# Attention kernel: both halves' weighted values together, projection in the fourth score bank

## What is computed

```python
def reference(x, ...):                      # x: (32, 96, 16, 16), float32
    x = _L0_conv_ref(x, ...)                # windowed attention, then an MLP
    return _L1_conv_ref(x, ...)             # channel attention

def _L0_conv_ref(x, qkv_w, qkv_b, proj_w, proj_b, rel_bias, ...):
    xn = _layernorm(x, norm1_g, norm1_b)    # over the 96 channels
    xs = jnp.roll(xn, shift=(-SS, -SS), axis=(1, 2))
    qkv = (xw @ qkv_w + qkv_b)...           # xw: 4 windows of 64 tokens per image, 12 heads of 8
    attn = jnp.einsum('bhnd,bhmd->bhnm', q * SCALE, k) + bias + mask
    attn = jax.nn.softmax(attn, axis=-1)
    out = jnp.einsum('bhnm,bhmd->bhnd', attn, v)...
    out = out @ proj_w + proj_b
    x = shortcut + jnp.roll(xs, shift=(SS, SS), axis=(1, 2))
    h = _layernorm(x, norm2_g, norm2_b)
    h = jax.nn.gelu(h @ fc1_w + fc1_b, approximate=False)
    return x + (h @ fc2_w + fc2_b)

def _L1_conv_ref(...):                      # layer norm over the image, 3x3 grouped convolutions
    ...                                     # to Q, K, V, 8 heads of 12 channels, softmax over
                                            # channels, a 1x1 projection and the normalised x
```

## Time and profile before

| | before |
|---|---|
| median of 3 executions | 552.92 us (550.82 to 564.15) |
| the profiled execution | 551.77 us, of which span 549.8 us |
| PE busy | 505.5 us (92%) |
| DVE busy | 337.8 us (61%) |
| ACT busy | 310.2 us (56%) |
| POOL busy | 176.7 us (32%) |
| mean granted TensorE clock | 0.97 of full speed |

### The profile page before, as it was taken

How to read it: one execution, slowest core, us unless ns; L and a number is a source line. 1 busy time by engine, 2 the same in 40 slices (tenths; PEclk the granted TensorE clock), 3 DMA queues, 4 the chain that set the end, 5 groups by cost and what they waited for, 6 DMA issues and landing times. The chain is left out here.

```text
span 549.8 us, 27773 instructions
## 1 busy us (share of the span) xinstructions
PE 505.5 (92%) x11496; PEld 337.2 (61%) x11496; DVE 337.8 (61%) x875; ACT 310.2 (56%) x763; POOL 176.7 (32%) x217
## 2 busy tenths in 40 slices
PE   7789999999999999999799999939999999999996
PEld 6767667667666666767575433219665565656553
DVE  1158888888888888887602473356456656566544
ACT  1138888888888888886533655302444444444432
POOL 8224444443333344444220202003353323333200
PEclk9779999999999999999999999977999999999998
DMA  3111111111111111100031132322464444434411
GB/s 76 25 49 33 32 31 42 26 26 25 29 29 29 29 29 29 29 4 4 1 82 37 39 88 66 96 61 55 113 167 112 110 121 118 113 105 114 120 50 30
DMA packets 40899, 32.62 MB, mean 59 GB/s; under 512 B 18954, under 2 KB 36491, under 8 KB 40843
## 3 DMA queue, kind: packets, MB, share of 16 engines
q1 hardware_dynamic: 37258, 26.11, 18.8%
q0 software_dynamic: 3584, 5.72, 4.7%
HBM read 18.36 MB, written 7.13 MB: 46 GB/s over the span
## 5 line engine op out<-in xcount | busy, mean ns | idle before, releaser
L391 POOL TENSOR_TENSOR scores<-scores,peak 128x768 f32<-128x768 f32 x64 | 92.9, 1473 | 148.1 <-DVE peak L555 148.1
L1235 POOL DMA_DIRECT2D x_stack<-padded_x x96 | 52.4, 548 | 96.3 <-PE ps_v L1508 59.8
L454 ACT COPY probs_t<-ps_probs 128x768 f32<-128x768 f32 x64 | 51.1, 799 | 18.8 <-PE ps_out L733 9.4
L548 DVE TENSOR_TENSOR scores<-ps_scores,bias 128x1536 f32<-128x1536 f32 x32 | 55.3, 1727 | 6.3 <-PE ps_scores L706 6.2
L716 PE MATMUL ps_probs<-ident,scores 128*128 128x128 f32 x384 | 55.9, 282 | 0.1
L555 DVE TENSOR_REDUCE peak<-scores 128x24 f32<-128x1536 f32 x32 | 55.8, 1744 | 0.1
L448 ACT ACTIVATE scores<-scores 128x768 f32<-128x768 f32 x64 | 54.2, 847 | 0.4 <-POOL scores L391 0.4
L733 PE MATMUL ps_out<-v_blocks,probs_t 128*32 128x18 f32 x3072 | 38.9, 187 | 15.2 <-DVE stream L574 15.1
L733 PEld LDWEIGHTS ps_out<-v_blocks,probs_t 128*32 128x32 f32 x3072 | 32.5, 110 | 31.5 <-issue 17.6
L1048 ACT ACTIVATE hidden<-ps_hidden,fc_b_folded 128x512 f32<-128x512 f32 x48 | 29.1, 688 | 36.5 <-PE ps_hidden L989 36.5
L1508 PE MATMUL ps_qk<-x_stack,conv_w 40*32 40x256 f32 x1536 | 48.8, 379 | 0.0
(11 more groups left out here) (159 smaller groups left out, 907.2 us busy)
## 6 DMA issues: line engine op xcount, KB each, us to landing
x_stack<-padded_x SPq DMA_DIRECT2D x96, 54.0 KB
x_stack<-padded_x POOLq DMA_DIRECT2D x96, 54.0 KB, 2.8
padded_x<-x_pad SPq DMA_DIRECT2D x32, 121.5 KB, 2.7
x_sliced<-stream SPq DMA_DIRECT2D x48, 64.0 KB, 2.0
mixed<-y_sliced SPq DMA_DIRECT2D x48, 64.0 KB, 2.0
out<-y_sb SPq DMA_DIRECT2D x32, 96.0 KB, 2.0
x_now<-in_x SPq DMA_DIRECT2D x32, 72.0 KB, 1.8
stream<-in_x SPq DMA_DIRECT2D x32, 72.0 KB, 1.9
```

What stands on the lines that cost most here:

```text
L391: nc.gpsimd.tensor_tensor(sc, sc, peak[:, par, p, :].unsqueeze(2).to_broadcast((128, HEADS, WN)), ALU.subtract).then_inc(s["shifted"], 1)
L454: nc.scalar.copy(probs_t[:, :], ps_turned).then_inc(s["turned_copied"], 1)
L548: nc.vector.tensor_tensor(scores[:, par, :, :].rearrange("p a (g c) -> p a g c", g=NG), ps_scores[:, :, 0:PAIRS * TRIO * WN].rearrange("p ...
L1235: engine.dma_start(x_stack[64 * half + i * HC:64 * half + (i + 1) * HC, slot, :, :], rows).then_inc(landed[slot], 16)
```

## The change

Five things are edited, all in `window_attention`.

- `probs_t` gets two buffers, one for each pair, and `copy_turned` waits one `weigh` less.
- Both halves of an image's `weigh` stand together at the end of PE's step t - 1, behind `project` and `turn_tokens`. Before, the second half stood in step t behind `score`. `turn_heads(t)` moves up to the place behind the first `turn`.
- `ps_proj` moves to bank 3 of `ps_scores`. With it, `weigh` no longer waits for a residual; `score(t)` waits until `residual_done` has reached t - 2, which in step t is the residual of image t - 1. `project` and `make_v` have further waits for the last images only.
- On DVE, `weigh_heads(t)` moves ahead of `add_bias(t + 2)`. The statistics are taken one step sooner, `measure(t + 5)` behind `copy_k(t + 3)`, and `add_residual(t)` follows them, at the end of step t. Before, the same residual stood near the start of step t + 1.
- On ACT, the second `exponent` moves ahead of the first `copy_turned`, and `copy_ot` ahead of `copy_q`.

The number and the sizes of the compute instructions stay as they are. Only the residual and the projection use another bank.

```diff
--- before.py
+++ after.py
@@ -246,7 +246,7 @@
     v_blocks = sb("v_blocks", [128, 2, PAIRS, 2, HP, 2, VC])
     scores = sb("scores", [128, 2, PAIRS, SC])
     peak = sb("peak", [128, 2, PAIRS, HEADS])
-    probs_t = sb("probs_t", [128, SC])
+    probs_t = sb("probs_t", [128, PAIRS, SC])
     recip = sb("recip", [128, PAIRS, HEADS])
     heads_out = sb("heads_out", [128, PAIRS, C])
     out_t = sb("out_t", [C, 2, N])
@@ -260,7 +260,7 @@
     ps_folded = ps_scores[0:C, 2, 0:3 * C]
     ps_q, ps_k = (ps_scores[:, g, 0:N] for g in range(2))
     ps_v = ps_scores[:, 2, 0:2 * C].rearrange("p (w q d) -> p w q d", w=2 * PAIRS, d=HD)
-    ps_proj = ps_out[0:C, 0, N:2 * N]
+    ps_proj = ps_scores[0:C, 3, 0:N]
     ps_turned = ps_probs.rearrange("p b c -> p (b c)")[:, 0:SC]
     ps_pv = ps_out[:, 0, 0:PAIRS * HEADS * VC].rearrange("p (a h c) -> p a h c", h=HEADS, c=VC)
     ps_ot = ps_out[0:C, 0, N:2 * N].rearrange("p (a n) -> p a n", a=PAIRS)
@@ -450,8 +450,8 @@
         def copy_turned(t, p):
             u = t * 2 + p
             act.wait_ge(s["turned"], u + 1)
-            need(act, s["pv_ready"], u)
-            nc.scalar.copy(probs_t[:, :], ps_turned).then_inc(s["turned_copied"], 1)
+            need(act, s["pv_ready"], u - 1)
+            nc.scalar.copy(probs_t[:, p, :], ps_turned).then_inc(s["turned_copied"], 1)
 
         def copy_ot(t, par):
             act.wait_ge(s["ot_ready"], t + 1)
@@ -473,15 +473,14 @@
                 inverse_deviation(t + 4)
                 scale(t + 4)
             if real(t + 1):
+                exponent(t + 1, 1, 1 - par)
                 copy_turned(t + 1, 0)
             if is_image(t, B - 2):
                 copy_tokens(nc, act, m, s2, 0, by_blocks(first_homes[0]))
-            if real(t + 1):
-                exponent(t + 1, 1, 1 - par)
+            if real(t):
+                copy_ot(t, par)
             if real(t + 3):
                 copy_q(t + 3)
-            if real(t):
-                copy_ot(t, par)
             if real(t + 2):
                 copy_v(t + 2, par)
             if real(t + 4):
@@ -568,7 +567,7 @@
                                     ALU.mult).then_inc(s["heads_ready"], 1)
 
         def add_residual(t, half, par):
-            dve.wait_ge(stream_in[1 - par], half * 32 if par == 0 else (half + 1) * 32)
+            dve.wait_ge(stream_in[par], (half + 1) * 32)
             dve.wait_ge(s["proj_ready"], t + 1)
             dst = stream[:, bass.ds(t * N, N)]
             nc.vector.scalar_tensor_tensor(out=dst, in0=ps_proj, scalar=b_proj[:, 0:1], in1=dst,
@@ -589,21 +588,15 @@
 
         def step(t, half, par):
             if real(t + 4):
-                measure(t + 4)
-                await_stats(t + 4)
-            if real(t - 1):
-                add_residual(t - 1, half, par)
-            if real(t + 4):
                 gather_spread()
             if is_image(t, -4):
                 prepare()
+            if real(t):
+                weigh_heads(t)
             if real(t + 2):
                 add_bias(t + 2, par)
             if is_image(t, B - 2):
                 measure_tokens(nc, dve, m, s2, 0, by_blocks(first_homes[0]))
-            if real(t):
-                weigh_heads(t)
-            if is_image(t, B - 2):
                 measure_tokens(nc, dve, m, s2, 1, by_blocks(first_homes[1]))
             if is_image(t, B - 1):
                 for k in range(QUARTERS, 2 * QUARTERS):
@@ -614,6 +607,11 @@
                 set_up_projection()
             if real(t + 3):
                 copy_k(t + 3)
+            if real(t + 5):
+                measure(t + 5)
+                await_stats(t + 5)
+            if real(t):
+                add_residual(t, half, par)
             if is_image(t, B - 2):
                 measure_tokens(nc, dve, m, s2, 2, by_blocks(first_homes[2]))
                 dve.wait_ge(weights_in, 16 * LATE)
@@ -684,6 +682,8 @@
                              skip_group_check=True).then_inc(s["k_ready"], 1)
 
         def make_v(t, par):
+            if past(t + 1):
+                pe.wait_ge(s["biased"], B)
             heads = w_qkv[:, 2 * WIDE:2 * WIDE + C].rearrange("c (q e d) -> c q e d", e=2, d=HD)
             for window in range(2 * PAIRS):
                 for part in range(PARTS_W):
@@ -696,6 +696,7 @@
 
             pe.wait_ge(s["q_copied"], t + 1)
             need(pe, s["v_copied"], t * 2)
+            need(pe, s["residual_done"], t - 2)
             pe.wait_ge(s["k_copied"], t + 1)
             for p in range(PAIRS):
                 for g in range(NG):
@@ -724,14 +725,12 @@
             if p == 0:
                 pe.wait_ge(s["v_copied"], (t + 1) * 2)
                 need(pe, s["ot_copied"], t * PAIRS)
-            else:
-                need(pe, s["residual_done"], t)
             pe.wait_ge(s["turned_copied"], u + 1)
             for q in range(HP):
                 for part in range(PARTS_W):
                     at = q * 128 + 32 * part
                     mm = nc.tensor.matmul(ps_pv[32 * part:32 * part + 32, p, 2 * q:2 * q + 2, :],
-                                          probs_t[:, at:at + 32], v_blocks[:, par, p, part // 2, q, :, :],
+                                          probs_t[:, p, at:at + 32], v_blocks[:, par, p, part // 2, q, :, :],
                                           start=True, stop=True, skip_group_check=True)
             mm.then_inc(s["pv_ready"], 1)
 
@@ -743,6 +742,8 @@
 
         def project(t, par):
             pe.wait_ge(s["ot_copied"], (t + 1) * PAIRS)
+            if past(t + 2):
+                need(pe, s["residual_done"], t)
             nc.tensor.matmul(ps_proj, w_proj[:, :], out_t[:, par, :], start=True, stop=True,
                              skip_group_check=True).then_inc(s["proj_ready"], 1)
 
@@ -795,10 +796,10 @@
                 score(t + 2)
             if is_image(t, -2):
                 fold_v()
-            if real(t):
-                weigh(t, 1, par)
             if real(t + 1):
                 turn(t + 1, 0, 1 - par)
+            if real(t):
+                turn_heads(t)
             if is_image(t, -4):
                 fill(nc, free, blank[:, :], 8)
             if real(t + 4):
@@ -809,8 +810,6 @@
                 fill(nc, free, blank[:, :], 6)
             if real(t + 3):
                 make_q_and_k(t + 3, 1 - par)
-            if real(t):
-                turn_heads(t)
             if real(t + 2):
                 make_v(t + 2, par)
             if is_image(t, B - 2):
@@ -825,11 +824,13 @@
                 fold_fc1(2)
             if real(t + 1):
                 turn(t + 1, 1, 1 - par)
-                weigh(t + 1, 0, 1 - par)
             if real(t):
                 project(t, par)
             if real(t + 5):
                 turn_tokens(t + 5, half + 2 + par, 1 - par)
+            if real(t + 1):
+                weigh(t + 1, 0, 1 - par)
+                weigh(t + 1, 1, 1 - par)
             if is_image(t, -2):
                 fill(nc, free, blank[:, :], 6)
 
@@ -838,7 +839,7 @@
         fill(nc, free, blank[:, :], 10)
         pe.wait_ge(turning_in, 16)
         led_image_loop(pe, step)
-        fill(nc, ps_scores[0:C, 3, 0:C], blank[:, :], 16)
+        fill(nc, ps_out[0:C, 0, 0:C], blank[:, :], 16)
         for c in range(SLICES):
             turn_first_slice(c)
```

## The result

| | before | after |
|---|---|---|
| median of 4 executions each | 554.5 us (550.82 to 564.15) | 575.62 us (573.45 to 575.79) |
| ratio, 95% interval | | 1.0395 [1.0326, 1.0464] |
| span of the profiled execution | 549.8 us | 573.7 us |
| PE busy | 505.5 us (92%) | 506.0 us (88%) |
| DVE busy | 337.8 us | 344.5 us |

A ratio leaves out executions more than 1.5% above the fastest of their kernel (here the one of 564.15 us), so that it is not the ratio of the two medians.

A forecast was written before the change was run, and what follows sets the result against it. It took a loop over PE and DVE (tokens, statistics, residual, `weigh`) as the bound; loop 6.6, unrolled images 1.6, start 0.7 and end 0.5 sum to 9.4 us more, forecast 561.5 us, range 554 to 568.

The forecast's parts named there:

- The tail: End of windowed attention: MLP statistics stand behind a residual they used to precede; +0.5 us, between -0.3 and +1.
- What bounds the kernel before: Loop before the change: tokens, statistics, residual and `weigh` close a loop over PE and DVE; 7.166 us an image.
- The bubble moves to the bias: Between scores and queries on PE: the 0.54 us wait at `weigh` goes, a new one of at least 0.37 us comes.
- The closed chain: Looped images: scores now wait for the residual behind the statistics; 7.44 us an image against 7.166, 6.6 us in the loop.
- Project to tokens: Chain term on PE, from `project` to `turn_tokens`: 0.51 us.
- Residual to scores: Chain term from DVE's residual, with the way to PE, to the next scores: 0.54 us.
- The signs that the prediction named: Scores wait for the residual some 30 times, about 0.35 us each; queries wait for the bias 0.4 to 0.5 us.
- What hides the rest: In the loop: early `weigh_heads` costs nothing, DVE cover 0.35 us; ACT's turned copy stays hidden, cover 0.27 us.
- The unrolled images: Five steps outside the loop, images 0, 1 and 26 to 28: +0.33 us each, 1.6 us.
- the head: Start of windowed attention: the first image's second `weigh` stands ahead of a score, 0.56 us plus a copy wait; +0.7 us.
- The clock: Rival: two PE bubbles an image bring half clock in the loop, 3 us more an image, over 600 us; chance 0.03.
- The third: Rival: extra conditions and register instructions around scores, bias and reciprocal make 7.65 us an image, 566 us; chance 0.24.

The follow-up runs named there:

- the version with early tokens: Kernel before with tokens' transposes ahead of the first weigh, normed copy ahead of values, statistics sooner, residual and gather ahead of the bias: 549.46 us, ratio 0.9756.
- four costs removed: Changed kernel with residual ahead of statistics, normed copy ahead of values, idle matmuls at the tail, four images per loop turn: 559.16 us, ratio 1.0050.
- the runs without this wait: Changed kernel with the residual ahead of the statistics (565.17 us), and further versions of it, such as four images per loop turn (565.66 us).
- the second weigh back: Changed kernel with PE's order and the reciprocal's place put back, second half's weigh again behind the scores: 583.34 us, ratio 1.0544.
- its long loop: Kernel before with four images in a turn of the loop in place of two: 554.40 us, ratio 1.0008.

## Why the prediction was wrong, step by step

The direction and the chain were right; the sum was 14.4 us short (9.4 for 23.8, both on the profiled executions). Two steps failed. The tail, "+0.5, between -0.3 and +1", measured 5.5: it priced late statistics and not the idle time and the clock behind them. The chain, "The sum is 7.44 us", measured 7.64: `project` to `turn_tokens` and the residual to the scores were too short, 4.7 us over the loop. The start gave 2.2 us more than summed in this profile (in its repeat 1.0 less) and the later stages 2.4 where nothing was put; for these the cause stays open.

**What bounds the kernel before: right.** The loop over tokens, statistics, residual and `weigh` was the limit; the version with early tokens broke it and took 0.23 us from each image (with the statistics sooner and the normed copy first).

**The bubble moves to the bias: right.** Scores to queries was put at 2.92 us; it is 2.91 (107.17 to 110.08). Neither the loss of the cover nor its return (3.00 us) moves it. The Trainium skill, "Perfetto Trace Analysis", section "Optimization Strategy", has repeated bubbles as a possible sign of too few buffers; by the earlier trace rows that rule promised 6.63 us an image. The runs disagree: with both buffers and the fourth bank in place and four costs removed, the image takes 7.206 us. The bubble stood at a buffer, and its cause was an order of instructions.

**The closed chain: right in kind, mis-sized in two terms.** Against the sum, start to start, with the mean over the two kinds of image:

| term | predicted | measured |
|---|---|---|
| scores to queries | 2.92 | 2.91 |
| queries to values | 1.03 | 1.03 |
| values to the second turn | 0.47 | 0.48 |
| turn to project | 0.81 | 0.71 |
| project to tokens | 0.51 | 0.70 |
| tokens to statistics | 0.41 | 0.45 |
| statistics to residual | 0.75 | 0.66 |
| residual to scores | 0.54 | 0.70 |
| sum | 7.44 | 7.64 |

- *Project to tokens, 0.51 us.* The prediction took it from the earlier trace rows as if PE alone decided it. It had the copies on ACT in hand, 0.71 and 0.43 us, and used them for the turned copy only; that `copy_normed` must also free `ps_a` for the tokens it did not ask. The kernel with the normed copy first shows the term: 0.26 us less at the tokens, 0.19 less an image.
- *Residual to scores, 0.54 us.* It was read at a `weigh` in the middle of a step. The scores open the step, and in every second image the turn of the loop as well, where it measures 0.83 us and not 0.58. That the 0.25 more is the loop's branch is an inference from the runs without this wait, where 0.44 to 0.64 us stay before the same images and move with the branch. Before, the same branch lay mostly under other work.

The signs that the prediction named came, and larger than put: the scores wait 27 times for 0.47 us each (0.35), the queries 30 times for 0.77 us (0.4 to 0.5), since PE's work between scores and queries ends after 2.15 us and not 2.55 (107.17 to 109.32).

The two mis-sized terms make 0.35 us, the other six give 0.15 back: 0.20 us an image, 4.7 of the 14.4 us missed.

**What hides the rest: right, and with little to spare.** ACT's turned copy releases no `weigh` in the loop of after, and `weigh_heads` ahead of the bias costs nothing (0.53 and 0.36 us idle ahead of the bias). The cover of 0.27 us on ACT was about used up once the chain was shortened: with the normed copy first, the second `weigh` waits for the turned copy.

**The unrolled images, +1.6 us, and the head, +0.7 us: a little too small.** Behind the loop it is 1.1 us, as forecast. Up to the loop it is 3.6 in one profile of the changed kernel and 0.4 in the other (1.9 in it from the first scores on), where 1.4 was summed (0.7 and two times 0.33). Of the difference between the two, 1.8 us lie ahead of the first scores (29.68 and 27.84). Behind them part is the clock: in the profile of after the fills before the second scores run at half clock, 2.13 us for 1.18 before the change.

```profile
36.76 2.13 PE L114 MATMUL ps_probs<-blank 96*96 96x96 f32 x12
38.82 1.49 PE L707 MATMUL ps_scores<-k_blocks,q_sb 32*64 32x192 f32 x32
```

**The tail, put at +0.5 us and measured at 5.5: the largest miss.** The step named the right instructions, the MLP statistics behind a residual, and priced them as work. It did not ask how long PE then stands still, nor what its clock does. The clock was a rival, with 0.03, but sought in the loop, where it stayed at 1.00. Its defence, came from a stretch in which PE still did 0.60 us of work in 2; at the tail it did none for 2.69. And that stretch was no defence. Its last 1.40 us PE stood idle, and the trace of before has half clock behind it:

```profile
35.99 0.36 PE L667 MATMUL ps_a<-ident,x_now 96*128 96x96 f32 x2 [1.40 <-ACT normed L425]
...
38.00:40.00 2.00, 2.00 (x28) 1.45 (x15) 1.24 (x1) 0.33 (x2) 0.00 (x0) 0.50 0.26 61
```

(The first is of the timeline, the second of the windows view.) The 1.41 us that the prediction took for scores at half clock were so only in part; the window from 36 to 38 us shows 0.89.

**The rest, +2.4 us in the later stages, was put at nothing.** Their code is the same. Both profiles have one stretch of some 14 us at half clock at the start of channel attention; in after's it ends about 0.7 us later against the work, and 0.7 of the 2.4 us arise there. The other 1.7 come behind it, at full clock. Over the profiles here the two stages took from 274.8 to 278.9 us, without order in what had been changed. I count it as chance, and have no run that shows it.

**The rivals.** The third, waits that cost more in new places, gave 566 us by three conditions in front of the scores. It had the right place and the right period (7.65), by another mechanism: no run points to the conditions. That its number lies nearest is luck. The price at the tail was in no rival.

## What to carry to other kernels

When a wait is moved to another instruction, list everything that this instruction waits for in its new place, each engine that reads the buffer it writes, and the branch if it opens a loop's turn. Price a late instruction at the tail by the idle time that it leaves on PE, since a fall of the clock can cost more than the wait. And where a bubble repeats at a buffer, look first for the instruction whose earlier issue shortens the chain: taking the tokens' transposes ahead of one `weigh`, with the statistics and the copy that follow from it, took 0.23 us from each image (a ratio of 0.976 to 0.984), where a second buffer and another bank with the order of this change gave nothing.

## What the runs showed of the hardware that I had not expected

- **The turn of a loop left PE idle for 0.44 to 0.64 us where nothing hid it.** It shows in full behind 48 short `weigh` matmuls (96 rows in 1.03 us), not at all behind 0.85 us of idle matmuls after them, and not behind a projection (the version with early tokens). Behind 24 short `weigh` matmuls no such time was seen either (the second weigh back), while a wait for the residual stood there. That the queue cannot run ahead of many short matmuls is my reading of it; how deep the queue is no run shows. The Trainium skill, "Advanced Engine Details and Errata", section "Control Flow Timing", gives about 51 ns for a branch and 108 ns for one that compares; the trace's 0.48 us, which is for the whole turn of a loop with its register instructions, is over four times that, and decides here. "Runtime: NRT & Kernel Launch", section "Instruction fetch mechanics", of the same skill says that a taken branch outside of the fetched window waits for a fetch; no run here tells that from other costs of a turn.
- **2.5 to 2.7 us of idle PE ahead of the last heads brought half clock in all eight profiles that have it** (after and seven of the experiments), for 10 to 14 us, and from the heads to the MLP it took 15.2 to 16.9 us for 10.4. An idle time of 0.64 and 0.81 us brought it in the profile of the version with early tokens, and not in three profiles whose tail is that of the kernel before (it, its repeat, its long loop).
- **Work without use can be worth its time**: 2.6 us of idle matmuls where PE had to wait anyway gave about 5 us back (574.13 to 568.82 us).
